# A decoder layer on one core: one PSUM bank changes hands, and the small parts of attention change step

## What is computed

```python
x = layernorm(x + self_attention(x))        # learned relative bias, NEG beyond distance 100
x = layernorm(x + cross_attention(x, ctx))  # causal
x = layernorm(x + moe(x))                   # 64 experts, 8 of 64 in 4 of 8 groups, plus shared
# attention: softmax(q k^T * scale + bias) v, then the output projection
# moe: sum over chosen experts of weight * relu(x up_w)^2 down_w, plus relu(x sh_up)^2 sh_down
```

## Time and profile before

| | |
|---|---|
| median of 3 runs | 298.11 us (297.36 to 299.08) |
| profiled execution, its own time | 299.01 us |
| its span, first to last instruction | 297.2 us |
| PE busy | 259.1 us (87%) |
| ACT busy | 218.3 us (73%) |
| DVE busy | 201.8 us (68%) |
| POOL busy | 140.6 us (47%) |
| mean granted clock of PE | 0.985 |

### The profile page before, as it was taken

The page is one execution under the profiler, slowest core; times in us unless marked ns, Lnnn a source line. Parts: engine busy times, 40 slices in busy tenths (PEclk is TensorE's granted clock), DMA queues, the critical chain, the costliest instruction groups (busy, mean ns, idle before and its releaser), DMA issues.

```text
span 297.2 us, 6022 instructions
## 1 busy us (share of the span) xinstructions
PE 259.1 (87%) x1912; PEld 203.1 (68%) x1912; DVE 201.8 (68%) x556; ACT 218.3 (73%) x593; POOL 140.6 (47%) x135
## 2 busy tenths in 40 slices
PE   4989999899999988888878549989998999999980
PEld 2589998677777765666655426458876888788860
DVE  2698736777777778666799993477897556845424
ACT  7462651877777789999889666778788888698850
POOL 4018003300011149574560000559999898699970
PEclk9999999999999999999999997999999999999996
DMA  6609310797323215666640000685664497496201
GB/s 121 170 9 412 105 44 4 176 275 227 99 64 90 83 39 123 162 181 174 172 132 2 0 3 3 158 201 164 197 169 120 124 234 194 127 241 183 85 0 35
DMA packets 52243, 37.94 MB, mean 128 GB/s; under 512 B 15794, under 2 KB 43124, under 8 KB 52212
## 3 DMA queue, kind: packets, MB, share of 16 engines
q1 hardware_dynamic: 52212, 37.57, 46.8%
HBM read 30.48 MB, written 7.08 MB: 126 GB/s over the span
## 4 chain that ended last, share of the span: by engine, by line
PE 54%; ACT 12%; POOL 12%; issue 10%; DVE 8%; DMA 1%; POOLq 1%; SPq 0%; DVEq 0%; ACTq 0%
PE bank L718 16%; POOL unit_lo L629 12%; PE bank L702 10%; PE bank L753 7%; ACT probs L980 6%; PE bank L763 5%; PE bank L735 4%; ACT probs_t L989 3%; PE bank L651 2%; PE bank L741 2%; PE bank L658 1%; DVE neg_max L1208 1%; DMA x_tok<-in_x 1%; PE bank L646 1%; PE bank L861 1%
## 5 line engine op out<-in xcount | busy, mean ns | idle before, releaser
L629 POOL TENSOR_TENSOR unit_lo<-unit,unit_hi 128x512 fp32r<-128x512 f32 x68 | 86.8, 1301 | 40.7 <-ACT unit_hi L1072 39.4
L980 ACT ACTIVATE probs<-bank,neg_max 128x128 f32<-128x128 f32 x256 | 73.2, 393 | 5.1 <-DVE neg_max L1208 4.9
L1339 DVE SCALAR_TENSOR_TENSOR scaled<-bank,roots 128x512 f32<-128x512 f32 x64 | 43.8, 687 | 28.7 <-PE bank L718 24.3
L1208 DVE TENSOR_REDUCE neg_max<-bank 128x4 f32<-128x512 f32 x64 | 43.9, 687 | 24.8 <-PE bank L741 20.9
L753 PE MATMUL bank<-ident,probs 128*128 128x128 f32 x256 | 39.9, 279 | 18.6 <-ACT probs_t L989 15.5
L1071 ACT ACTIVATE unit<-scaled 128x512 f32<-128x512 f32 x68 | 42.8, 630 | 17.5 <-DVE scaled L1339 17.0
L753 PEld LDWEIGHTS bank<-ident,probs 128*128 128x128 f32 x256 | 28.4, 141 | 28.7 <-ACT probs L980 17.4
L1072 ACT ACTIVATE unit_hi<-scaled 128x512 fp32r<-128x512 f32 x68 | 42.0, 617 | 0.0
L741 PE MATMUL bank<-k_bd,q_stk 128*128 128x512 f32 x64 | 34.0, 531 | 0.0
L702 PE MATMUL bank<-spread,rel_t 128*128 128x128 f32 x256 | 28.9, 275 | 0.0
L702 PEld LDWEIGHTS bank<-spread,rel_t 128*128 128x128 f32 x256 | 28.7, 192 | 0.1
(11 more groups left out here) (199 smaller groups left out, 462.5 us busy)
## 6 DMA issues: line engine op xcount, KB each, us to landing
roots<-root_dram SPq DMA_DIRECT2D x60, 256.0 KB, 4.5
q_stk<-q_dram SPq DMA_DIRECT2D x16, 128.0 KB, 3.0
k_bd<-k_dram SPq DMA_DIRECT2D x32, 64.0 KB, 2.6
incoming<-in_L_ffn_up_w SPq DMA_DIRECT2D x4, 512.0 KB, 4.9
q_stk<-qc_dram SPq DMA_DIRECT2D x16, 128.0 KB, 3.2
k_bd<-kc_dram SPq DMA_DIRECT2D x32, 64.0 KB, 2.5
incoming<-in_L_ffn_down_w SPq DMA_DIRECT2D x4, 512.0 KB, 4.1
k_dram<-k_hi SPq DMA_DIRECT2D x2, 512.0 KB, 3.4
```

The source lines that it names most:

```text
L629: nc.gpsimd.tensor_tensor(unit_lo[:, k % R], unit[:, k % 3], unit_hi[:, k % R], ALU.subtract).then_inc(lo_ready, 1)
L980: last = nc.scalar.activation(probs[:, U % 3, h4 * L:(h4 + 1) * L], ps[BS[U % 3]][:, h4 * L:(h4 + 1) * L], ACT.Exp, bias=neg_max[:, U % 4, ...
L1208: nc.vector.tensor_reduce(neg_max[:, U % 4, :], ps[BS[U % 3]][:, :].rearrange("p (h j) -> p h j", h=GH), AX.X, ALU.max, negate=True).then_ ...
L1339: ins = nc.vector.scalar_tensor_tensor(scaled[:, k % 3], h, 0.0, roots[:, n % ROOT_RING, c % ROOTS], ALU.max, ALU.mult)
```

## The change

1. `BS` gets bank 7 as a fourth bank, so `scores(U)` waits for exps of stage U-4 where it waited for stage U-3.
2. `turn_outputs` writes bank `BX`, where the projection writes too; `turn_tokens` writes `BM`, with `back` and `use_tokens`. The waits follow the new owners.
3. `turned_out` on ACT moves from offset 8 to 9. `layer_norm` moves from 11 to 12, `turn_tokens` and `tokens_out` from 12 to 13, `use_tokens` and `queries_out` from 13 to 14. The first two groups' routing starts one step later (51 and 59 for 50 and 58), since it counts from `USE`; the first transpose of weights comes in step 65 for 64.
4. Within a step PE does `turn_tokens` ahead of `transpose_probs`, and `output_projection` behind it. DVE does `layer_norm` right behind `normalise`, and `residual` behind `probs_out` (it was ahead). ACT does `turned_out` and `tokens_out` first, and `log_variance` after `probs_out`.
5. The routing of the third group waits for the last exps (bank 7 is its scratch), no longer for the last `turned_out`.

```diff
-GATHERED, BACK, TURN, TURNED, PROJ, LOG, NORM, TOKENS, USE = 6, 8, 9, 8, 10, 10, 11, 12, 13
+GATHERED, BACK, TURN, PROJ, LOG, NORM, TOKENS, USE = 6, 8, 9, 10, 10, 12, 13, 14
-BS, BX, BP, BO, BM, BN = (1, 4, 0), 2, 3, 5, 6, 7
+BS, BX, BP, BO, BM, BN = (1, 4, 0, 7), 2, 3, 5, 6, 7
             def scores(U):
-                b, r, bank = B % NB, B % RING, ps[BS[U % 3]]
+                b, r, bank = B % NB, B % RING, ps[BS[U % 4]]
-                if U >= 3:
-                    pe.wait_ge(exp_done, U - 2)
+                if U >= 4:
+                    pe.wait_ge(exp_done, U - 3)
             def turn_outputs(B):
                 if B >= 1:
-                    pe.wait_ge(ont_out, B)
-                nc.tensor.transpose(ps[BN][:, 0:128], o_norm[:, B % 2, :], ident[:, :]).then_inc(ont_ready, 1)
+                    pe.wait_ge(mom_ready, B)
+                nc.tensor.transpose(ps[BX][:, 0:128], o_norm[:, B % 2, :], ident[:, :]).then_inc(ont_ready, 1)
             def output_projection(B):
                 pe.wait_ge(ont_out, B + 1)
-                if B >= 1:
-                    pe.wait_ge(mom_ready, B)
-                if B >= 1:
-                    pe.wait_ge(xt_out, B)
             def turn_tokens(B):
-                pe.wait_ge(mom_ready, B + 1)
-                nc.tensor.transpose(ps[BX][:, 0:D], src, ident[:, :]).then_inc(xt_ready, 1)
+                pe.wait_ge(on_ready, min(B + 2, 2 * NB))
+                nc.tensor.transpose(ps[BM][:, 0:D], src, ident[:, :]).then_inc(xt_ready, 1)
             def use_tokens(B):
-                pe.wait_ge(on_ready, min(B + 2, 2 * NB))
-                if B >= 1:
-                    read_tokens(B - 1)
...
                 if at_step(s, TURN) is not None:
                     turn_outputs(at_step(s, TURN))
+                if at_step(s, TOKENS) is not None:
+                    turn_tokens(at_step(s, TOKENS))
+                if 0 <= s - LT < STAGES:
+                    transpose_probs(s - LT)
                 if at_step(s, PROJ) is not None:
                     output_projection(at_step(s, PROJ))
-                if 0 <= s - LT < STAGES:
-                    transpose_probs(s - LT)
-                if at_step(s, TOKENS) is not None:
-                    turn_tokens(at_step(s, TOKENS))
...
                 k = s - MOE0
-                if at_step(s, LOG) is not None:
-                    log_variance(at_step(s, LOG))
+                if at_step(s, TURN) is not None:
+                    turned_out(at_step(s, TURN))
...
                     probs_out(s - LT)
+                if at_step(s, LOG) is not None:
+                    log_variance(at_step(s, LOG))
                 if at_step(s, GATHERED) is not None:
                     outputs_out(at_step(s, GATHERED))
-                if at_step(s, TURNED) is not None:
-                    turned_out(at_step(s, TURNED))
...
                     if q == 2:
-                        dve.wait_ge(ont_out, 2 * NB)
+                        dve.wait_ge(exp_done, STAGES)
...
                     normalise(at_step(s, BACK))
+                if at_step(s, NORM) is not None:
+                    layer_norm(at_step(s, NORM))
+                if 0 <= s - LT < STAGES and probs_by_vector(s - LT):
+                    probs_out(s - LT)
                 if at_step(s, PROJ) is not None:
                     residual(at_step(s, PROJ))
-                if 0 <= s - LT < STAGES and probs_by_vector(s - LT):
-                    probs_out(s - LT)
-                if at_step(s, NORM) is not None:
-                    layer_norm(at_step(s, NORM))
```

More of the change, by code:

```diff
@@ L825, in turn_weights @@
                     pe.wait_ge(exp_done, STAGES - 2)
-                else:
-                    pe.wait_ge(ont_out, 2 * NB)
                 for n in range(HB):
@@ L980, in exps @@
                     last = nc.scalar.activation(probs[:, U % 3, h4 * L:(h4 + 1) * L],
-                                                ps[BS[U % 3]][:, h4 * L:(h4 + 1) * L], ACT.Exp,
+                                                ps[BS[U % 4]][:, h4 * L:(h4 + 1) * L], ACT.Exp,
                                                 bias=neg_max[:, U % 4, h4:h4 + 1])
@@ L1000, in turned_out @@
                     act.wait_ge(proj_ready, B - 1)
-                nc.scalar.copy(on_t[:, B % 2, :], ps[BN][:, 0:128]).then_inc(ont_out, 1)
+                nc.scalar.copy(on_t[:, B % 2, :], ps[BX][:, 0:128]).then_inc(ont_out, 1)
             def log_variance(B):
@@ L1023, in tokens_out @@
                 if B >= NB:
-                    nc.scalar.copy(x2_hi[:, b * L:(b + 1) * L], ps[BX][:, 0:D])
-                nc.scalar.copy(dst, ps[BX][:, 0:D]).then_inc(xt_out, 1)
+                    nc.scalar.copy(x2_hi[:, b * L:(b + 1) * L], ps[BM][:, 0:D])
+                nc.scalar.copy(dst, ps[BM][:, 0:D]).then_inc(xt_out, 1)
             def queries_out(B):
@@ L1207, in maxima @@
                     dve.wait_ge(exp_done, U - 3)
-                nc.vector.tensor_reduce(neg_max[:, U % 4, :], ps[BS[U % 3]][:, :].rearrange("p (h j) -> p h j", h=GH),
+                nc.vector.tensor_reduce(neg_max[:, U % 4, :], ps[BS[U % 4]][:, :].rearrange("p (h j) -> p h j", h=GH),
                                         AX.X, ALU.max, negate=True).then_inc(max_ready, 1)
```

## The result

The changed kernel takes **295.94 us** (median of 20 runs, 295.02 to 297.23); the kernel before, measured beside it, 298.52 (20 runs, 296.01 to 300.36). The ratio is 0.9923, with a 95% interval of 0.9902 to 0.9944, so the gain is 2.3 us by the ratio (the medians lie 2.6 apart), a little more than the 0.5% that can be told from no change. The forecast was 297.4, the range 294.0 to 301.5. The profiled execution's own time is 296.53 (before 299.01), its span 294.7 (297.2).

What follows compares the result with a forecast made beforehand. PE was taken to bound self attention, ACT cross attention, then DVE from step 52. -0.8 + 1.7 + 0.3 - 1.9 = -0.7 us gave 298.3 from 299.01, or 297.4 on the median's scale; range 294.0 to 301.5.

Steps and rivals of the forecast that it cites:

- fourth bank: Scores in attention: the old wait for exps of stage U-3 could never be the last one, so 0 us.
- steps 8 to 32: Self attention: ACT's stall at `turned_out` goes, a batch takes 7.67 us for 7.84, together -0.8 us.
- steps 32 to 48: Cross attention: ACT waits about 0.9 us before `log_variance`, batches take 8.06, then 8.23 us, together +1.7 us.
- steps 48 to 60: Late cross attention: two plain batches cost 0.6 more each, the 9.23 us one falls to 8.3, together +0.3 us.
- seam: End of attention to experts: roots come 1.4 us later, but PE hides 3.3 us of work under DVE's routing, -1.9 us.
- expert part: Experts behind attention: shifted as a whole, its own moved instructions hidden under the roots' copies, 0 us (0.5 either way uncovered).
- the bank's rival: PE's holes before transposes in attention and at the seam vanish with the extra bank: -8 us, so 290 (half: 294); chance 0.12.
- the loop: Attention: T(0), copy(0), `residual`, `log_variance`, exps(2), T(2) wait in a circle; 7.67 us a self batch, 8.06 to 8.23 a cross batch.
- The residual's loop at a higher price: Rival at ACT's `log_variance`: a wait of 1.4 us for 0.9 makes the change +3.6, so 301.7 us; chance 0.2.
- The seam giving nothing: Rival at the end of attention: T(63) still stands behind `first_roots`, 0 for -1.9, so 299.3 us; chance 0.12.
- The idle time at `on_t`: Sign on ACT in self attention: idle time before `on_t` falls from 1.22 to below 0.5 us.
- the wait at `ln_var`: Sign on ACT in cross attention: 0.7 to 1.0 us idle before `log_variance`, released by DVE's moments.

## Why the prediction was right, and where it was off

The forecast's case came, on its better side: 295.94 for 297.4, inside its own range of 295.3 to 299.5, with the sign and the mechanism as argued. Of the three outcomes it was faster, which had 0.34, and not the one within 0.5%, which had 0.44. The gain was about three times the 0.7 forecast. Three of the four sizes were off, by 0.7 to 1.0 us and not all the same way, so it is in part luck that the sum lies no further off. The differences from before to after, by the table:

| term | forecast | measured |
|---|---|---|
| fourth bank | 0 | 0 |
| steps 8 to 32 | -0.8 | -1.76 |
| steps 32 to 48 | +1.7 | +1.02 |
| steps 48 to 60 | +0.3 | +0.08 |
| seam | -1.9 | -1.05 |
| expert part | 0 | +0.02 (-2.49 to -2.47) |
| sum | -0.7 | -1.7 |

Stage 0 also began 0.78 earlier in the profile after, in code that is the same; by the scatter of that number the profiles cannot tell whether any of it is real. The -1.7 lies at the edge of what the ratio allows (-1.7 to -2.9), so up to a microsecond stays without a place.

- **The bank: right**, for the reason given. Three pairs of kernels with and without it agree, and the wait of the transposes, which comes first, was there all the time. (The medians with four banks are 0.8 lower, the same within 0.1 and 0.6 lower in these pairs, each time inside the intervals; no stretch of attention shows a difference over 0.08 where both are undisturbed.) With that the bank's rival falls, and with it the reading of the repeated gap as a lack of PSUM: the gap was 4.5, 3.5 and 3.8 us of waits on ACT in the earlier trace rows's stretch that the bank left as they were and one moved instruction removed.
- **Self attention: mechanism right, the term mis-sized.** I had 7.67 for the loop; it is 7.55 (T(0) to T(2) 4.09 for 4.18, T(2) to T(3) 2.09 for 2.06, to the next T(0) 1.37 for 1.43). The 0.12 would be the five hand-overs, estimated at 0.05 to 0.15, each a few hundredths too long; no row tells them apart. The larger miss is the first batch: "nothing much in the first, which has no tokens yet". It fell from 7.55 to 7.02, since it had ACT's stall all the same: 1.72 us before `on_t` at 64.91, and 0.53 after the change. That is -0.53 of the -0.96 missing.
- **Cross attention: right, but for where it starts.** Forecast 8.06, then 8.23; measured 8.02, 8.02, 8.14, and from step 48 on 8.19, 8.19, 8.18. The step that failed is that I charged the first cross batch too: steps 32 to 36 took 7.58 for 7.80, a gain of 0.22 where I had a loss of 0.38. The loop as I added it up has three copies on ACT, and between steps 30 and 34 DVE still makes two of them, since stages 29 and 30 are self attention's; that this is the reason wasn't tried.
- **Steps 48 to 60: the size right, the reason partly wrong.** The batches give +0.56, -1.04, +0.56 for my +0.6, -0.9, +0.6. `r_one` took 0.22, as in "under 1 us", but not because it starts behind 148.0: it started at 146.07, just as `w_lo` ended (at 146.11), as POOL began it 1.88 earlier. "POOL's work keeps its place" fails. Nor does the length of the batch hang on it. In the kernel after with three banks POOL was not yet through, `r_one` took 1.34, and the batch was 8.20, as long as the 8.19 without the blocking. What made it 8.2 is that DVE is no longer the engine that sets the batch there (6.61 busy of 8.19, for 8.52 of 9.23): a blocking of a microsecond fits into its slack. That rests on this one pair of profiles.
- **The seam: mechanism right, a half of the size.** Step 60 to the roots: forecast 17.3, measured 179.17 - 162.10 = 17.07. From there PE should have hidden 3.3, and hid 2.25. Of the 1.8 priced between the roots and `turn_weights` only 0.1 went (1.66 for 1.77): T(62) and its products do stand ahead of the roots now, but the first expert unit and T(63) came in their place. From `turn_weights` to `root_out` it is 4.35 for 6.49, so 2.1 went where I had 1.5. T(62), T(63) and the products between ran at half clock until 181 (1.09, 1.06 and 1.04, where the same products take 0.62 at 182.56), and PE was busy without a break from 176.12 until `turn_weights` at 180.83. At full clock these 4.7 us would be about 2.4 and done before the roots at 179.17: an estimate from these lengths, if nothing else held PE up.
- **The rivals.** The residual's loop at a higher price would have shown 1.1 us or more at `ln_var`; it was 0.76 to 0.85 in cross attention. The seam giving nothing needed T(63) behind the first roots; it came at 179.98, ahead of `turn_weights`.
- **The signs.** The idle time at `on_t`, the wait at `ln_var` and `r_one` came as stated, and the cross batches but for the first (7.58). Two signs were missed narrowly: the self batch is 7.55, below 7.6 to 7.75, and the first `root_out` comes 185.18 - 162.10 = 23.08 after step 60 begins, above 22 to 23.

What I did not see is how good the change could have been. I took ACT's stall for a loss in self attention alone; moved by itself it is worth 6.2 us, and by its profile (a run 1.2 below its median) 3.1 are saved in self attention, 1.6 and 1.2 in cross attention and 1.4 at the seam. With the other moves, but without the loop, 9.7 are saved, and the loop takes 7.4 of them back. My forecast of a small net gain was the difference of two larger numbers, each of them too small.

## What to carry to other kernels

Before a buffer is added, look at the other waits of the same instruction queue: a wait that an earlier instruction has already stood for, to the same count, cannot be the last, and its buffer buys nothing. A small copy that stands one step ahead of the work that feeds it can cost every engine of a pipeline; compare the place of each waiting instruction with the place of its producer, and move it first, alone. When several instructions are moved at once, run each move by itself: here one was worth 6.2 us, and two others cost 7.4 together, measured within the change. And look at PE's granted clock in every run before a move near a seam is called worthless.

## What the runs showed of the hardware

**TensorE's clock falls at the end of attention in every profile here, and in three of them twice.** Windows of 2 us of the kernel after (us, PE, PEld, DVE, ACT, POOL busy, granted clock, DMA, GB/s):

```profile
172.00:174.00 2.00, 0.63 (x4) 0.42 (x4) 1.86 (x8) 0.40 (x2) 0.00 (x0) 1.00 0.02 4
174.00:176.00 2.00, 1.12 (x4) 0.72 (x4) 1.90 (x9) 2.00 (x8) 0.00 (x0) 0.56 0.00 0
176.00:178.00 2.00, 1.88 (x20) 1.17 (x20) 1.75 (x8) 1.80 (x7) 0.00 (x0) 0.50 0.03 8
178.00:180.00 2.00, 2.00 (x10) 1.50 (x7) 1.08 (x4) 0.59 (x2) 0.00 (x0) 0.50 0.00 0
180.00:182.00 2.00, 2.00 (x12) 1.84 (x11) 0.49 (x1) 1.57 (x5) 0.00 (x0) 0.74 0.00 0
```

PE has little to do before 174 (0.63 of 2 us, the longest idle time 1.51 us), and then its clock goes to half, which is 1.2 of 2.4 GHz, just as the work comes back. In the kernel before it was so from 178 to 183, in the one with `turned_out` alone from 162 to 168. In the kernels before with the routing one step later, alone or with `turned_out`, and in the one with the bank alone, it falls a second time. The same view of the first of these:

```profile
182.00:184.00 2.00, 1.21 (x20) 0.71 (x18) 1.24 (x4) 1.53 (x5) 0.84 (x1) 1.00 0.00 0
184.00:186.00 2.00, 1.58 (x4) 0.80 (x5) 0.45 (x2) 2.00 (x6) 0.43 (x1) 0.96 0.22 51
186.00:188.00 2.00, 2.00 (x4) 0.58 (x3) 0.69 (x1) 0.85 (x2) 1.27 (x1) 0.50 0.07 18
188.00:190.00 2.00, 2.00 (x4) 1.05 (x4) 0.00 (x0) 1.30 (x3) 1.21 (x1) 0.50 0.75 224
190.00:192.00 2.00, 2.00 (x7) 1.36 (x6) 0.69 (x3) 0.43 (x2) 0.07 (x1) 0.50 1.00 232
```

From 186 to 192 PE is busy all the time at half clock, and between unit 0 and unit 3 it loses 3.2 us to the kernel before, more than steps 48 to 60 and the seam had won. Only one run of each kernel has a profile, but each has its mean granted clock, and those of this kernel are in two groups (0.988 to 0.991 and 0.960 to 0.979). In the profile, at 0.976, the second stretch costs 3.4 us of full clock, by the clocks of its windows from 184 to 194 (that of 192 to 194 is 0.84); without it the mean would be 0.976 + 3.4 / 299.5 = 0.987, an estimate that meets the upper group. So the second fall probably comes in about half of its runs, and costs more than the edit gains. No profile of a run of the upper group shows it gone. I had treated the seam as a matter of order; the clock sets what is left of a gain there.

**DVE waits out POOL's instructions at their whole length.** `r_one` takes 0.22 us undisturbed; in the kernel with the bank alone it met `w_lo` at its start (144.94 to 147.31), and took 2.34, until 147.39:

```profile
145.05 2.34 DVE L1258 TENSOR_SCALAR r_one<-r_exp 128x128 f32<-128x128 f32 x1
```

Its batch took 10.39 us, for 9.23 before, and that is nearly all of the 1.2 by which its steps 48 to 60 are longer. But only 0.2 of it is the blocking (2.34 for 2.16). The rest came from the clock, which fell here in the middle of attention too, behind 1.30 us in which PE stood idle for `layer_norm`; in the kernel before, with 1.12 us of the same wait, it stayed at 1.00. The windows of the kernel with the bank alone:

```profile
148.00:150.00 2.00, 0.70 (x13) 0.51 (x17) 2.00 (x6) 0.97 (x4) 0.00 (x0) 0.90 0.76 224
150.00:152.00 2.00, 2.00 (x18) 1.29 (x11) 1.55 (x12) 1.17 (x5) 0.71 (x1) 0.50 0.81 230
152.00:154.00 2.00, 1.72 (x9) 1.46 (x8) 1.03 (x6) 1.92 (x8) 1.92 (x2) 0.74 0.38 107
```

In the kernel after it is `layer_norm` that pays: 1.15 us at 123.09, 1.56 at 131.12 and 1.13 at 139.26, each until 0.08 or 0.09 behind the end of an instruction of POOL, for 0.34 at 148.29, where POOL is idle. Two, the first of these and the 2.51 at 131.94 in the kernel with the later routing alone, even start 0.03 and 0.07 ahead of POOL's instruction by the records, which are rough for POOL. So a difference of a microsecond in one stretch of a single profile can come from where POOL's work happens to fall, as there. No run took POOL's work away, so that the two block each other is read from where they end together, and isn't tried by itself.
